# The experts' loop of a fused block: the next tile's rows are turned ahead of the up product, SP issues a load ahead of the older store, and Pool asks for expert 5 before it splits expert 4

## What is computed

```python
probs = jax.nn.softmax(xt @ W_router, axis=-1)
top_v, top_i = jax.lax.top_k(probs, K_TOP)                 # K_TOP = 2
gate = jnp.sum(jax.nn.one_hot(top_i, E_rt, dtype=xt.dtype) * top_v[..., None], axis=1)
rt_mid = jax.nn.gelu(jnp.einsum('th,ehd->ted', xt, Wrt_up), approximate=False)
routed_out = jnp.einsum('ted,edh->th', rt_mid * gate[:, :, None], Wrt_down)
return (shared_out + routed_out).reshape(B, S, H)
```

## Time and profile before

| | us |
|---|---|
| median of 3 runs (lowest, highest) | 936.26 (936.14, 937.33) |
| profiled execution, its own time | 932.21 |
| its span, first to last instruction | 930.4 |
| experts' loop, first to last tile | about 720 to 875 |
| PE busy | 887.3 (95% of the span) |
| DVE, ACT, POOL busy | 523.6, 383.0, 387.1 |
| mean granted TensorE clock | 0.990 of full speed |

### The profile page before, as it was taken

How to read it: one execution, slowest core, us unless ns; L and a number is a source line. 1 busy time by engine, 2 the same in 40 slices (tenths; PEclk the granted TensorE clock), 3 DMA queues, 4 the chain that set the end, 5 groups by cost and what they waited for, 6 DMA issues and landing times.

```text
span 930.4 us, 13567 instructions
## 1 busy us (share of the span) xinstructions
PE 887.3 (95%) x4264; PEld 714.8 (77%) x4265; DVE 523.6 (56%) x999; ACT 383.0 (41%) x632; POOL 387.1 (42%) x282
## 2 busy tenths in 40 slices
PE   6899879999998999999999999999999999999995
PEld 2467658878776888888888888888887888878874
DVE  5798797998667111263226522651496444444388
ACT  2666565583735533322232223225443333333252
POOL 3331200100022546316301630268537699888584
PEclk9999989999999999999999999999999999999998
DMA  9657578566056327487213421466435789786787
GB/s 354 214 150 230 198 234 264 162 201 215 1 171 218 131 93 237 145 261 260 91 35 129 143 91 35 137 216 225 159 115 183 243 259 275 270 270 204 248 245 173
DMA packets 121824, 174.03 MB, mean 187 GB/s; under 512 B 8216, under 2 KB 69656, under 8 KB 118704
## 3 DMA queue, kind: packets, MB, share of 16 engines
q1 hardware_dynamic: 58896, 111.55, 35.4%
q0 software_dynamic: 9216, 34.61, 12.1%
q10 hardware_dynamic: 53664, 27.26, 10.4%
HBM read 97.58 MB, written 75.81 MB: 186 GB/s over the span
## 4 chain that ended last, share of the span: by engine, by line
PE 76%; DVE 7%; DMA 5%; POOL 4%; issue 4%; ACT 2%; SPq 0%; DVEq 0%; ACTq 0%; POOLq 0%
PE kk_ps L426 6%; PE kv_ps L426 6%; PE kk_ps L428 6%; PE kv_ps L428 6%; PE kk_ps L427 6%; PE kv_ps L427 6%; PE mm_ps L426 6%; PE mm_ps L428 6%; PE mm_ps L427 6%; PE up_ps L426 3%; POOL g1b L2567 2%; DMA xsb<-xs_s 2%; PE up_ps L427 2%; PE up_ps L428 2%; PE dn_ps L428 2%
## 5 line engine op out<-in xcount | busy, mean ns | idle before, releaser
L1569 DVE TENSOR_TENSOR silu<-kk_ps,silu 128x512 fp32r<-128x512 f32 x64 | 44.3, 692 | 198.5 <-ACT silu L2238 197.9
L2234 ACT ACTIVATE kk_ps<-kk_ps 128x512 f32<-128x512 f32 x64 | 37.2, 582 | 207.2 <-PE kk_ps L428 207.2
L426 PE MATMUL kk_ps<-xk,cm_w 128*128 128x512 f32 x256 | 100.8, 394 | 0.0
L426 PE MATMUL kv_ps<-cm_w,silu 128*128 128x512 f32 x256 | 100.5, 393 | 0.0
L428 PE MATMUL kk_ps<-xk,cm_w 128*128 128x512 f32 x256 | 99.8, 390 | 0.0
L428 PE MATMUL kv_ps<-cm_w,silu 128*128 128x512 f32 x256 | 99.7, 390 | 0.0
L427 PE MATMUL kk_ps<-xk,cm_w 128*128 128x512 f32 x256 | 99.6, 389 | 0.0
L427 PE MATMUL kv_ps<-cm_w,silu 128*128 128x512 f32 x256 | 99.6, 389 | 0.0
L2404 POOL TENSOR_TENSOR cm_w<-stage,cm_w 128x1024 fp32r<-128x1024 f32 x16 | 38.7, 2426 | 88.3 <-ACT cm_w L2019 72.5
L1896 DVE TENSOR_TENSOR xsT<-xs_ps,xsT 128x512 fp32r<-128x512 f32 x42 | 29.1, 692 | 75.7 <-ACT xsT L2321 75.6
L2411 POOL TENSOR_TENSOR rs<-mv,neghalf 128x4 f32<-128x4 f32 (+2 forms) x13 | 13.5, 1039 | 133.8 <-DVE mv L1279 133.7
(11 more groups left out here) (298 smaller groups left out, 2338.5 us busy)
## 6 DMA issues: line engine op xcount, KB each, us to landing
xs_s<-zero ACTq DMA_DIRECT2D x13, 1024.0 KB, 6.2
ys_s<-zero ACTq DMA_DIRECT2D x13, 1024.0 KB, 6.4
xsb<-xs_s SPq DMA_DIRECT2D x44, 256.0 KB, 3.4
ys_s<-ysb SPq DMA_DIRECT2D x41, 256.0 KB, 3.6
ex_raw<-in_wex POOLq DMA_DIRECT2D x9, 1024.0 KB, 6.7
stage<-in_wcm SPq DMA_DIRECT2D x16, 512.0 KB, 4.0
wmod<-in_wmod SPq DMA_DIRECT2D x6, 1024.0 KB, 12.2
ex_raw<-in_wex SPq DMA_DIRECT2D x6, 1024.0 KB, 7.7
```

What stands on the lines that cost most here:

```text
L426: pe.matmul(out, lhs[0], rhs[0], start=first, stop=False)
L1569: dve.tensor_tensor(silu[:, g % NSILU, 1, :], kk_ps[g % 2][:, :], silu[:, g % NSILU, 0, :].bitcast(F32), ALU.subtract).then_inc(s_silo, 1)
L2234: act.activation(kk_ps[g % 2][:, :], kk_ps[g % 2][:, :], ACT.Silu).then_inc(s_silu, 1)
```

## The change

`turn_x` moves ahead of `up` in both halves of the loop, and ACT's copy of the turned rows ahead of the gelu, to match. DVE's order stays. SP issues the load of a tile ahead of the store that is one older than before. Pool asks for expert 5 before it splits expert 4, and for expert 6 only behind the split of expert 5; from expert 6 on its order is the old one.

```diff
@@ SP
             load_ht(NB - 1)
+            load_xs(4, 0, 3)
+            load_xs(5, 1, 4)
+            store_y(0, 0, 1 + AHEAD)
             def pair(i):
                 load_xs(i * 2 + 4, 0, i * 2 + 3)
+                store_y(i * 2 - 1, 1, i * 2 + AHEAD)
+                load_xs(i * 2 + 5, 1, i * 2 + 4)
                 store_y(i * 2, 0, i * 2 + 1 + AHEAD)
-                load_xs(i * 2 + 5, 1, i * 2 + 4)
-                store_y(i * 2 + 1, 1, i * 2 + 2 + AHEAD)
...
-            with sp.Fori(0, pairs) as i:
+            with sp.Fori(1, pairs) as i:
                 pair(i)
+            store_y(pairs * 2 - 1, 1, pairs * 2 + AHEAD)
@@ PE
             def pair(i, w0, w1):
+                turn_x(0, i * 16 + 32)
                 up(w1, slot_of(w1), 1, i * 2 + 2)
-                turn_x(0, i * 16 + 32)
                 down(slot_of(w0), 0, i * 2 + 1, i * 2 + 1)
                 w2 = word_of(i * 2 + 2)
                 turn_m(1, i * 2 + 2)
+                turn_x(1, i * 16 + 32)
                 up(w2, slot_of(w2), 0, i * 2 + 3)
-                turn_x(1, i * 16 + 32)
                 down(slot_of(w1), 1, i * 2 + 2, i * 2 + 2)
@@ ACT
+                turned_hi(0, i * 2 + 3)
                 gelu4(1, i * 2 + 2)
-                turned_hi(0, i * 2 + 3)
                 turned_mid_hi(1, i * 2 + 2)
+                turned_hi(1, i * 2 + 4)
                 gelu4(0, i * 2 + 3)
-                turned_hi(1, i * 2 + 4)
                 turned_mid_hi(0, i * 2 + 3)
@@ POOL
             expert_load(PRE)
             ht_lo(2)
+            expert_load(PRE + 1)
             expert_split(PRE)
-            expert_load(PRE + 1)

             for e in range(PRE + 1, NE):
-                if e + 1 < NE:
+                if PRE + 1 < e < NE - 1:
                     expert_load(e + 1)
                 expert_split(e)
+                if e == PRE + 1:
+                    expert_load(e + 1)
```

## The result

| | before | changed |
|---|---|---|
| median, us | 936.80 (936.14 to 938.12, 4 runs) | 949.76 (946.69 to 953.18, 4 runs) |
| ratio | | 1.0125, 95% interval 1.0099 to 1.0152 |
| profiled execution, its time and span | 932.21, 930.4 | 946.69, 944.9 |
| mean granted clock of that execution | 0.990 | 0.977 |
| first scatter of Pool (unchanged code ahead of the loop) | 695.99 | 701.54 |

The kernel is 13 us slower there; I had forecast 935.8, no change. The pair of profiled executions lies 14.5 us apart, in three parts: 5.5 ahead of anything that the change touches, 3.0 in the loop, 6.0 behind it. So there are two questions: why the loop won nothing, and where the rest came from.

The account below looks back on a forecast made before the run. A closed ring (turn, ACT, DVE, `up`) was taken to leave PE empty 0.24 us of each 3.74 us tile. Summed: 0 at tile 32, -2.0 behind it, +1.5 for the store, so -0.5 us; median 935.8, range 933.2 to 939.3.

Parts of the forecast that it names:

- The gap before `up` closes: PE in the loop: the turn moved ahead of `up` removes 0.24 us of idle, so a tile takes 3.50 us, not 3.74.
- Pool: Pool's new order: load of expert 6 lands after 7.6 us, its split starts 2.4 us later, expert 13 ready at 838.8.
- the late landings: Loop, loads of experts 5 to 12: mean wait 0.9 us each, 7 us in all, PE still ahead of expert 13, costing nothing.
- my second rival: Loop: if waits exceed 1.1 us per expert's load, PE reaches tile 32 after its weights; at 1.6, end 939.5; chance 0.15.
- a cover of 5.6 us: Loop, SP's stores: time a store has to land before the `y_out` two tiles on; landings had taken up to 7.5 us.
- some 4 us: SP's store beside Pool's load: landing if DMA engines alternate queues by packet; the forecast used the rows' 7.5 us instead.
- Tile 32: First tile of expert 13: PE waits there for weights and begins at 838.9, as before, losing 31 tiles' gain.
- The wait at expert 13 costs clock: Rival: PE idle in one piece ahead of tile 32 brings 3.2 us at half speed, costing 1.6 us, 937.4; chance 0.12.
- Tile 37, its store and the end: Loop's end: `down` of tile 37 ends 2.0 us earlier, its store issues 2.35 us behind it, the kernel ends 0.5 us earlier.
- the 1.51 that I called the least: SP's queue: a load and a store in a row are at least 1.51 us apart, which delays the store of tile 37.
- Everything behind it is Pool's row of gathers and DVE's end, unchanged: Behind the landing of tile 37's store: the rest takes as long as before, so the kernel ends 0.5 us earlier.
- my forecast of no change within 0.2%: Whole kernel: median 935.8 us; 0.2% is 1.9 us, and staying within it had chance 0.48.

Follow-up runs that it names:

- e8: Changed kernel without the loads and splits of experts 9 to 15, using weights already in their slots; 932.07 us against 934.90 before, ratio 0.9973, chip Q.
- e10: Changed kernel, unchanged, timed again on chip R; 933.57 us against 933.87 before, ratio 1.0001.
- e6: Changed kernel, unchanged, for a second trace on chip Q; one run, 931.77 us against 934.90 before.
- e11: Changed kernel with an expert's load written as four 2 KB pieces a partition instead of 8 KB rows; 936.33 us against 933.87 before, ratio 1.0032, chip R.
- e15: Changed kernel, unchanged, timed once more on chip S; 936.08 us against 935.23 before, ratio 1.0021.
- e7: Changed kernel with Pool's first gather held until PE's fourth shared up tile of block 2; 952.18 us against 933.87 before, ratio 1.0178, chip R.
- e1: Kernel before with only SP's part of the change; 961.01 us against 938.28 before, ratio 1.0259, chip P.
- e2: Kernel before with only PE's and ACT's part of the change; 945.02 us against 938.28 before, ratio 1.0075, chip P.
- e3: Kernel before with only Pool's part of the change; 939.00 us against 938.28 before, ratio 1.0020, chip P.
- e16: Kernel of e14 timed again in more rounds on chip T; 938.67 us against 938.94 before, ratio 0.9985.
- e4: Changed kernel without Pool's part; 950.37 us against 938.28 before, ratio 1.0142, chip P.
- e14: Changed kernel with loads of rows on ACT's queue, SP issuing stores alone, Pool's order as before; 933.51 us against 935.23 before, ratio 0.9980, chip S.
- e17: Kernel of e1 timed again on chip T; 960.41 us against 938.94 before, ratio 1.0239.

## Why the prediction was wrong

**The gap before `up` closes.** Right: 3.48 us a tile where nothing else waits, 3.50 predicted; 3.45 in e8 behind the loads.

**Pool.** The mechanism was right and the size off. Less 5.55, the split of 4 began at 729.0 (728.1 predicted). The load of 6 was issued 752.52 - 5.55 = 746.97 (745.8) and landed 8.6 later, where I had taken 7.6, so the split of 6 was at 755.6 instead of 753.4 and expert 13 ready at 840.6 instead of 838.8: 4.1 us later than before, not 2.4. I had the load of 7 nowhere in this step; in the changed kernel it is issued 2.3 us behind that of 6.

**The step that failed in the loop is the late landings:** "I take a mean of 0.9, 7 us in all, which brings PE from 829.8 to 837: still ahead of expert 13, so it costs nothing." From tile 7 to 31 are 24 tiles, 83.4 us at 3.475. They took 94.8 to 96.7 in the four traces, so 11.4 to 13.3 are lost, of which weights are 2.7 in the first and 0.4 in e10, and the lower clock 1.7 in the first: about 1.1 us for each of the eight loads issued in that stretch (experts 7 to 14) in the first trace, and 1.4 to 1.7, with the clock's part in it, in the others. Before, the same 24 tiles lose 2.1 to 2.4 against 3.74 each. So 9 to 11 us of new waits stand against a gain of 24 x 0.26 = 6.4. This is my second rival, to which I gave 0.15, with its bound of 1.1 us a load reached in the first trace and passed in the others. The parts of it were in the text: a cover of 5.6 us against landings of 7.5. I had taken the largest landing of before for the largest; it was 9.0 here, where two loads ran at once (e6, above). I had also counted eight loads, of experts 5 to 12, ahead of tile 32; in the trace of before those of 13 and 14 are issued ahead of it too, at 815.45 and 827.59, and ten at my own 0.9 would have brought PE to 838.8 and used up the whole cover.

Here the Trainium skill, in "DMA: Bandwidth & Descriptors", section "Queues, rings and completion order", says more than I had read out of it: an engine drains a whole packet of one ring, typically 9 to 17 descriptors, before it turns to the next. An estimate from that page: an expert's load has 128 rows of 8 KB over 16 engines, 8 for each, and if a row is one descriptor, that is less than one such packet, so a store behind it can meet the whole of its share. The traces do not contradict it: the store issued at 784.96 in the kernel before landed 7.5 us later, at 792.5, and the load issued 0.35 us ahead of it landed 8.6 us behind its issue, at 793.2; in e6 landings of 8.3 and 9.0 stand beside loads that themselves took 8.7 and 13.6. None of them is near the "some 4 us" that I had worked out from half of the rate. How an engine groups the rows no run shows: what the profile counts as packets are the single rows of up to 8 KB, and e11, which would have tested it, left them as they were.

**Tile 32.** Predicted 838.9, measured 840.96. In the first trace the weights held PE there, as I had said, only 1.8 us later than I had said, because the load of 6 took 8.6 us instead of 7.6; the late landings had brought PE to 838.25 where I had 837. In e10 PE waited 0.4 us for the weights, in e6 and e15 not at all, and there the landings alone have eaten the gain.

**The clock.** "The wait at expert 13 costs clock" happened: PE idle for 2.72 us, less than the 3.23 of the earlier trace rows, then about 3.4 us at 0.50, so 1.7 us. Each of the four traces of the changed kernel has one such fall in the loop, in the other three behind a `y_out` that waited (e6 from 757 on); neither trace of before has one.

**Tile 37, its store and the end.** Its `y_out` was at 872.25 - 5.55 = 866.7, predicted 862.8, before 864.87. The store was issued at 874.05, 1.80 behind it, where before it was 0.86: right in kind, and 0.5 less than the 2.35 that I gave, since a load and a store in a row stand only 1.24 us apart there (872.81 and 874.05); the 1.51 that I called the least was not the least. The first gather came 3.0 us later where I had 0.5 earlier; in this pair that is tile 32's 2.1 and the clock's 1.7, less what the store was priced too high. That the end hangs on the gather is shown by e7.

**Ahead of the loop and behind it.** Most of the 13 us lie there. For the stretch behind the first gather the prediction says: "Everything behind it is Pool's row of gathers and DVE's end, unchanged". That step failed too, and by more than those in the loop: 68.2 us instead of 62.3. For the stretch ahead of the loop I had no step. There the scatter came between 695.62 and 701.54 in twenty traces, and at 696.25 to 701.54 in the four of the changed kernel. It goes with the clock in unchanged code. The two stretches of the first pair, before and changed:

```profile
100.00:200.00 100.00, 88.19 (x396) 72.58 (x397) 90.92 (x171) 62.28 (x97) 11.28 (x8) 0.95 0.66 202
200.00:300.00 100.00, 95.08 (x438) 77.42 (x437) 71.95 (x119) 55.83 (x88) 12.28 (x7) 1.00 0.48 155
```

```profile
100.00:200.00 100.00, 88.75 (x382) 72.56 (x381) 88.60 (x168) 59.42 (x92) 11.25 (x8) 0.90 0.63 198
200.00:300.00 100.00, 95.77 (x431) 77.79 (x430) 70.80 (x122) 56.53 (x89) 8.57 (x6) 0.97 0.48 153
```

The mean clock is lower by 0.05 and 0.03 over 100 us each, 8 us of full speed, where 5.5 us of time were lost. Which of PE's waits bring it about in one execution and not in the next I did not follow. The change does not bring this part with it, as the other three traces show; how much of it the medians hold is not known. Before's profiled execution was 4.6 us below its median, the changed one's 3.1.

The 6 us behind the gather go with the waits "remote". All seven traces on P and T have such waits and none of the eleven on Q, R and S has, so they go with the chip, or with the hour: each chip was used in one session only. The changed kernel is 1.0125 on the first and 1.0001 and 1.0021 on R and S, and e11 on R 1.0032. There my forecast of no change within 0.2% would have been right or at the edge (933.57 against 933.87, 936.08 against 935.23), and by luck: the gain went into late landings and not into a wait for expert 13.

Why the waits come where they do stays open. All stand behind a count that PE raises; by the Trainium skill, in "Perfetto Trace Analysis", section "Tensor Engine Instruction (MATMUL, LD_WEIGHTS)", the end of a matmul in a profile is estimated and the count follows the real one, so rows cannot tell a late matmul from a late count. Nor is it settled why the kernel before suffers so little: its median was 936.8 to 938.9 where such waits were seen and 933.9 to 935.2 on the others, only 1.6 to 5 us more, and the only trace of it that may be from such a chip has none. The sum of the waits does not order the losses: e1 has 14.0 us of them and lost 2.6%, e2 22.0 and lost 0.75%, e3 11.0 and lost 0.2%, e16 19.4 and lost nothing. The exits do in part: e1, e4 and their second timings, which have SP's new order with Pool's old one, took 74 to 77 us there, the other four traces with such waits 64 to 70. Neither of these two kernels was run on a chip like Q, R or S, so whether their long exits are the chip's or their own is not shown.

## What to carry to other kernels

When a loop with pairs of buffers gets faster, recount each transfer's time to land against two of the new, shorter tiles, with the longest landing beside the largest other transfer and not with a mean; a gain of 0.24 us a tile was smaller than the waits that its own speed and the new orders opened. Look, too, at what a moved load now stands next to: beside two loads 2.3 us apart two tiles lost over 4 us. Where a load and a store share one queue, an order between them only chooses which is late; a second queue (e14, e16) brought the waits from some 30 us or more to 17 and 19, and the whole to 0.998 and 0.9985 of before on two chips, each still inside its interval: no version here is shown to beat the kernel before. A difference of a per cent deserves a second chip before it deserves an explanation.

## What the runs showed of the hardware

- The same kernel pair was 1.0125 on one chip and 1.0001 and 1.0021 on two others, with intervals of 0.3% to either side. In the first pair's changed kernel and on two further chips, engines behind PE waited up to 16.94 us for a count whose matmuls' rows had ended (21.9 us before, in e17), and only behind the first gather.
- A 256 KB store that lands in 2.0 us alone took up to 7.5 beside one 1024 KB load of another queue in the kernel before, and 9.0 beside two of them issued 2.3 us apart, with two adding transfers of 256 KB between (e6).
- With the experts' loads written as four rows of 2 KB the execution had 3121 packets of 8 KB or more, exactly as many as with rows of 8 KB (e11, e10).
